# Last attention: head halves instead of key parities in the column tiles of the weighing

## The reference, cut to what matters

```python
q = (x @ Wq).reshape(b, n, 16, 64).transpose(0, 2, 1, 3) * scale
kv = x @ Wkv
k, v = (kv[..., :64], kv[..., 64:])
sim = jnp.einsum('bhid,bjd->bhij', q, k) + bias          # causal mask
attn = jax.nn.softmax(sim, axis=-1)
out = jnp.einsum('bhij,bjd->bhid', attn, v)              # the weighing
out = out.transpose(0, 2, 1, 3).reshape(b, n, 1024)
return out @ Wout + bout                                 # the projection
```

## Time and profile before

| | |
|---|---|
| median of 3 runs | 3847.4 us (3842.58 to 3852.38) |
| the profiled execution | 3845.26 us, span 3843.5 us |
| busy over the span | TensorE 83%, weight loads 45%, VectorE 62%, ScalarE 48%, GpSimd 24% |
| granted TensorE clock, mean | 0.898 |
| weighing, L2367 | 9216 MATMUL records, 324.0 us busy |
| projection of this layer, L2381 | 1024 MATMUL records, 144.0 us busy |
| norm, L2314 | 64 instructions, 151.1 us busy |

### The profile page before, as it was taken

One profiled execution on the slowest core, in us unless ns is written; L12 is line 12 of the kernel. 1 busy time (PEld: TensorE's weight loads), 2 busy tenths in 40 slices (PEclk: granted clock), 3 DMA queues, 4 the chain that ended last, 5 costly groups with the idle time before them and its releaser, 6 DMA issues. The chain is left out here.

```text
span 3843.5 us, 68233 instructions
## 1 busy us (share of the span) xinstructions
PE 3181.4 (83%) x25621; PEld 1748.6 (45%) x25621; DVE 2368.5 (62%) x5084; ACT 1844.5 (48%) x3309; POOL 921.2 (24%) x732
## 2 busy tenths in 40 slices
PE   5748888885759999797699969998888888889899
PEld 2213333331337655573222227763555444555676
DVE  5457777772656455564599942236778777778322
ACT  3214555553226423363289925434555555555444
POOL 1007888894100223000000000001121112212100
PEclk8668999997879899896599969998999988999999
DMA  4112323221033000132422210028444335432100
GB/s 146 41 51 72 106 76 103 79 91 31 12 93 132 2 1 1 45 133 79 144 58 67 68 35 1 1 81 219 122 122 101 108 103 128 122 103 82 31 9 12
DMA packets 229588, 289.46 MB, mean 75 GB/s; under 512 B 44861, under 2 KB 164121, under 8 KB 226950
## 3 DMA queue, kind: packets, MB, share of 16 engines
q1 hardware_dynamic: 229303, 285.61, 25.0%
HBM read 229.49 MB, written 56.55 MB: 74 GB/s over the span
## 5 line engine op out<-in xcount | busy, mean ns | idle before, releaser
L1169 POOL TENSOR_TENSOR l0aa_e<-l0aa_e,l0aa_et 128x512 f32<-128x512 f32 x432 | 538.1, 1274 | 139.1 <-ACT l0aa_e L1311 139.1
L2407 ACT ACTIVATE l1ba_sg<-l1ba_sg,l1ba_mn 128x128 f32<-128x128 f32 (+7 forms) x512 | 394.1, 771 | 303.4 <-DVE l1ba_mn L2451 302.4
L2451 DVE CUSTOM_DVE_ANT_0 l1ba_sg<-l1ba_pS,l1ba_tab 128x128 f32<-128x128 f32 (+7 forms) x512 | 369.0, 745 | 167.4 <-PE l1ba_pS L2347 90.1
L2347 PE MATMUL l1ba_pS<-l1b_k,l1ba_qs 64*128 64x448 f32 (+7 forms) x2048 | 372.2, 470 | 103.5 <-DMA l1ba_qs<-l1b_qd 64.9
L1342 DVE TENSOR_REDUCE l0aa_low<-l0aa_pP 128x8 f32<-128x1024 f32 x288 | 342.2, 1220 | 164.4 <-PE l0aa_pP L1193 163.6
L2460 DVE STREAM_TRANSPOSE l1ba_pT<-l1ba_sg 128x1024 f32<-128x1024 f32 (+3 forms) x344 | 367.1, 1067 | 35.7 <-PE l1ba_pO L2367 32.3
L1311 ACT ACTIVATE l0aa_e<-l0aa_pS 128x512 f32<-128x512 f32 x432 | 257.0, 595 | 259.5 <-PE l0aa_pS L1226 152.7
L2367 PE MATMUL l1ba_pO<-l1ba_pT,l1ba_v 32*64 32x256 f32 x9216 | 324.0, 397 | 5.5 <-ACT l1ba_y L2422 4.6
L319 PEld LDWEIGHTS f_pY<-l_w,f_hT 128*128 128x128 f32 x2048 | 268.1, 192 | 123.8 <-issue 118.8
L2314 POOL TENSOR_TENSOR l1ba_co<-l1ba_co,l1ba_rb 128x1024 f32<-128x1024 f32 x64 | 151.1, 2360 | 709.6 <-ACT l1ba_co L2415 676.7
L2817 ACT ACTIVATE l1aa_e<-l1aa_e 128x1536 f32<-128x1536 f32 x192 | 284.6, 1484 | 43.2 <-DVE l1aa_e L2858 25.9
(11 more groups left out here) (398 smaller groups left out, 5008.1 us busy)
## 6 DMA issues: line engine op xcount, KB each, us to landing
f_wB<-l0f_weights SPq DMA_DIRECT2D x16, 2048.0 KB, 7.2
l1ba_qs<-l1b_qd SPq DMA_DIRECT2D x128, 256.0 KB
l1ba_tab<-l1b_table SPq DMA_DIRECT2D x64, 512.0 KB
l1ba_rb<-l1b_rdd SPq DMA_DIRECT2D x64, 512.0 KB
l0aa_et<-l0a_table SPq DMA_DIRECT2D x16, 1536.0 KB
l1b_qd<-l1bp_part SPq DMA_DIRECT2D x64, 256.0 KB, 2.3
l0aa_et<-l0a_table SPq DMA_DIRECT2D x16, 512.0 KB
l0aa_qs<-l0a_qd SPq DMA_DIRECT2D x64, 96.0 KB
```

The costliest lines, as they stand in the source:

```text
L1169: nc.gpsimd.tensor_tensor(es, es, t, ALU.mult).then_inc(multiplied, 1)
L2347: ins = nc.tensor.matmul(pS[n % 2][:, at:at + half], qs[lo:lo + HALF, r % 2, i + k, :], ks[lo:lo + HALF, key:key + half], start=True, stop ...
L2407: nc.scalar.activation(row, row, ACT.Exp, bias=mn[:, r % 2, i + k:i + k + 1], scale=-1.0, accum_out=den[:, r % 2, i + k:i + k + 1]).then_i ...
L2451: nc.vector.tensor_tensor_reduce(row, scores, bias, 1.0, 3e38, ALU.add, ALU.min, mn[:, r % 2, h:h + 1]).then_inc(m_done, 1)
```

## The change

The column tiles of the weighing now hold two halves of the round's heads (0 to 3 and 4 to 7) and not two halves of the keys. Both column tiles take the same values and stream the 128 columns of their own four heads, so a key block takes 8 matmuls of 128 columns where a pair of key blocks took 8 of 256. `co` then has 4 head pairs of 128 columns instead of 8 heads, with one head of a pair on each half of the partitions. `rb` and `wo` follow: `rb` is loaded by two DMAs, one for each half of the partitions with that half's heads, and `wo` by four. The projection contracts a pair of heads in each of 4 matmuls. The pieces of the weighing are now counted in key blocks and not in pairs of them.

```diff
+    HP = HG // 2
-    def pairs(r):
-        return width(r) // Q // 2
+    def key_blocks(r):
+        return width(r) // Q
...
-        co, rb = sb("co", [P, 2, HG, P]), sb("rb", [P, HG, P])
+        co, rb = sb("co", [P, 2, HP, P]), sb("rb", [P, HP, P])
-        wo, bo = sb("wo", [P, 2 * HG, DIM]), sb("bo", [P, DIM])
+        wo, bo = sb("wo", [P, 2 * HP, DIM]), sb("bo", [P, DIM])
...
-                    sp.wait_ge(r_in, (r - 1) * 16)
+                    sp.wait_ge(r_in, (r - 1) * 32)
...
-                sp.dma_start(rb[:].rearrange("p h q -> p (h q)"), rdd[r % 2:r % 2 + 1].broadcast_to([P, HG * P])
-                             ).then_inc(r_in, 16)
+                for part in (0, 1):
+                    sp.dma_start(rb[part * HALF:(part + 1) * HALF].rearrange("p h q -> p (h q)"),
+                                 rdd[r % 2:r % 2 + 1, part * HP * P:(part + 1) * HP * P].broadcast_to([HALF, HP * P])).then_inc(r_in, 16)
...
-            for lo in (0, HALF):
-                sp.dma_start(wo[lo:lo + HALF], D["L1_attn_b_Wout"].rearrange("(h p) d -> p h d", p=HD)).then_inc(w_in, 16)
+            for hg in (0, 1):
+                for part in (0, 1):
+                    row = (hg * HG + part * HP) * HD
+                    sp.dma_start(wo[part * HALF:(part + 1) * HALF, hg * HP:(hg + 1) * HP],
+                                 D["L1_attn_b_Wout"][row:row + HP * HD, :].rearrange("(h p) d -> p h d", p=HD)).then_inc(w_in, 16)
...
-                for s in range(lo, hi):
+                for j in range(lo, hi):
                     for a in range(STRIPS):
                         for part in (0, 1):
-                            j = 2 * s + part
-                            ins = nc.tensor.matmul(pO[a][part * HALF:(part + 1) * HALF, 0:HG * Q],
+                            ins = nc.tensor.matmul(pO[a][part * HALF:(part + 1) * HALF, 0:HP * Q],
                                                    v4[a * Q:(a + 1) * Q, group_of(r)[0] % 2, (SEQ - width(r)) // Q + j, :],
-                                                   rows[a * Q:(a + 1) * Q, :, j * Q:(j + 1) * Q],
-                                                   start=(s == 0), stop=(s == pairs(r) - 1), skip_group_check=True)
+                                                   rows[a * Q:(a + 1) * Q, part * HP:(part + 1) * HP, j * Q:(j + 1) * Q],
+                                                   start=(j == 0), stop=(j == key_blocks(r) - 1), skip_group_check=True)
...
-                for h in range(HG):
-                    ins = nc.tensor.matmul(pO[BANKS[0]][:, 0:DIM], co[:, r % 2, h, :],
-                                           wo[:, group_of(r)[1] * HG + h, :], start=(h == 0), stop=(h == HG - 1), skip_group_check=True)
+                for k in range(HP):
+                    ins = nc.tensor.matmul(pO[BANKS[0]][:, 0:DIM], co[:, r % 2, k, :],
+                                           wo[:, group_of(r)[1] * HP + k, :], start=(k == 0), stop=(k == HP - 1), skip_group_check=True)
...
-                        weigh(r, (n - first) * pairs(r) // units, (n - first + 1) * pairs(r) // units)
+                        weigh(r, (n - first) * key_blocks(r) // units, (n - first + 1) * key_blocks(r) // units)
...
-                    nc.scalar.activation(co[:, r % 2, :, a * Q:(a + 1) * Q], pO[a][:, 0:HG * Q].rearrange("p (h q) -> p h q", q=Q),
+                    nc.scalar.activation(co[:, r % 2, :, a * Q:(a + 1) * Q], pO[a][:, 0:HP * Q].rearrange("p (h q) -> p h q", q=Q),
```

More of the change, by code:

```diff
@@ L2311, in norm @@
                 pool.wait_ge(o_out, STRIPS * (r + 1))
-                pool.wait_ge(r_in, (r + 1) * 16)
+                pool.wait_ge(r_in, (r + 1) * 32)
                 rows = co[:, r % 2].rearrange("p h q -> p (h q)")
@@ L2322, in add @@
                 nc.gpsimd.tensor_tensor(xs, xs, y[:, r % 2], ALU.add).then_inc(x_done, 1)
-            pool.wait_ge(w_in, 48)
+            pool.wait_ge(w_in, 80)
             rows = x[:, GROUP_BLOCKS:GROUP_BLOCKS + BLOCKS, :]
@@ L2362, in weigh @@
                 rows = pT[r % 2][:, 0:HG * width(r)].rearrange("p (h w) -> p h w", w=width(r))
-                for s in range(lo, hi):
+                for j in range(lo, hi):
                     for a in range(STRIPS):
                         for part in (0, 1):
-                            j = 2 * s + part
-                            ins = nc.tensor.matmul(pO[a][part * HALF:(part + 1) * HALF, 0:HG * Q],
+                            ins = nc.tensor.matmul(pO[a][part * HALF:(part + 1) * HALF, 0:HP * Q],
                                                    v4[a * Q:(a + 1) * Q, group_of(r)[0] % 2, (SEQ - width(r)) // Q + j, :],
-                                                   rows[a * Q:(a + 1) * Q, :, j * Q:(j + 1) * Q],
-                                                   start=(s == 0), stop=(s == pairs(r) - 1), skip_group_check=True)
-                if hi == pairs(r):
+                                                   rows[a * Q:(a + 1) * Q, part * HP:(part + 1) * HP, j * Q:(j + 1) * Q],
+                                                   start=(j == 0), stop=(j == key_blocks(r) - 1), skip_group_check=True)
+                if hi == key_blocks(r):
                     ins.then_inc(pv_done, 1)
```

## The result

The change made the kernel slower: 3877.1 us (median of 5 runs, 3866.1 to 3887.1) against 3845.5 us, a ratio of 1.0083 with a 95% interval of 1.0055 to 1.0112. The forecast was 3775 us, faster. The profiled execution of the changed kernel took 3877.07 us, span 3875.3.

The account below looks back on a forecast made before the run. TensorE was taken to bound the kernel, VectorE close behind; -67 + 6 + 3 - 3 - 12 - 4 + 5 = -72 us from 3845.3 gave 3773, forecast as 3775 us, range 3748 to 3835.

Parts of the forecast that it names:

- What bounds the kernel: TensorE fullest, VectorE next and level in wide units; the projection on the path by nearly its whole length.
- The projection: Projection on TensorE goes from 8 to 4 matmuls a round, 512 of its steps go: -67 us.
- The weighing: Twice the weighing records at half the columns; the wave halves to 0.108 us, sum stays 249 us: +3 us.
- 6.8 ns an instruction: Pace a half wave of the weighing needs, 16 instructions in 0.108 us; a burst's start showed 4.1 ns.
- The instruction rate sets the wave: Rival on the weighing: each of 9216 added records costs 27 ns on TensorE, +249 us, about 3990 us in all; 10%.
- a busy time of 300 us or more for the weighing: Sign on the weighing's line L2367: at this busy time the forecast is wrong by its main step; near 250 expected.
- The two rules of the Trainium skill: Rules against the weighing step: matmul starts at least about 25 ns apart, and an issue floor of some 20 cycles.
- The copies and the norm: Bank copies 0.1 us shorter each, -3 us; norm product 2.36 to 1.27 us; -12 us at groups, -4 at the end.
- -12 us at the group changes: At the start of 7 further head groups, shorter norm and smaller `rb` bring the table sooner: 1.7 us each.
- the 0.4 us that the forecast gave to the shorter copies: At each group change the norm starts 0.4 us sooner behind shorter bank copies.
- the most that the forecast gave to a smaller `rb`: At group changes, with DMA engines full, `rb` brings 0.25 MB less: between 0 and 1.0 us more.
- VectorE's wait for scores: Sign: VectorE's wait for scores from TensorE falls from 90 to about 40 us.

Follow-up runs that it names:

- rest_only: The changed kernel with the weighing of the kernel before (256 columns, half the instructions), all else as changed: 3779.5 us, ratio 0.981.
- split_only: The kernel before with every 256-column weighing matmul made into two of 128 columns, heads 0 to 3 then 4 to 7: 3966.5 us, ratio 1.0293.
- hy_wide: Mixed kernel: new layout in blocks 0, 1, 5, 6 and 7, layout before in 2, 3 and 4; measured level with the kernel before.

## Why the prediction was wrong, step by step

**What bounds the kernel** was right: TensorE's path with VectorE close behind, and rest_only's -66 us fits a projection that stood on it (its copies and norm shrank in the same run).

**The projection** was right in size: 144.0 to 77.2 us in rest_only, -67 as forecast.

**The weighing** is the step that failed: "If the stream sets the wave it halves to 0.108, and the sum stays at 249 us", at +3 us. The wave did halve in the median, to 0.109 us; the mean within bursts is 0.119, where the forecast had 0.109 with its 1 ns. The step failed one level above it: the sum of waves assumes that the instructions for them are there. I asked the right question, whether 6.8 ns an instruction can be held, and answered it with 22 instructions in 0.09 us. That is the rate at which TensorE takes instructions it already has. It says nothing of the rate at which they come from memory, and the half of the trace that does, the instruction queue in the DMA part of the profile, I read and did not use: one page per 7 to 8 us in the wide units before, 4.3 us at the least, twice that need after. That packets come no closer than 3.3 us could not be seen there, since the kernel before never reached it. What could be seen is that the change asks for 256 instructions per 1.74 us inside a burst (16 in 0.109), while the packet alone took about 1.1 us and nothing in the trace showed a shorter turn than 4.3 us. The rival "The instruction rate sets the wave" named the resource and had 10%. Its mechanism was wrong too: it is no slower rate everywhere, +249 us, but holes of 0.5 to 4 us at page ends. The prediction's own sign for this step, a busy time of 300 us or more for the weighing, came with 379.1, but it was set too low to say much: the kernel before has 324.0 for waves that sum to 249.

The two rules of the Trainium skill, by the earlier trace rows and now by the changed kernel: matmul starts at least 25 ns apart ("TensorE: Matmul & The Clock Gate", section "Wait — 56ns, not 53.3ns?") does not hold on 8 tiles, where undisturbed bursts come to 0.22 / 16 = 14 ns. "Runtime: NRT & Kernel Launch", section "Instruction fetch mechanics", says that a sequencer loads 16 KiB blocks of 256 instructions through its own DMA queue, and the 16384-byte packets agree. It also says that fetching stays hidden since dispatch is slower than the fill, and that fails here: TensorE took an instruction in some 4 ns, and 46 times in the changed kernel it stood empty until 2.3 to 3.1 us after the packet of its next page had started.

**What the holes cost.** Over rest_only the stretch of the changed kernel is longer by 949.5 - 841.9 = 107.6 us. The page-end residue holds 81.1 - 3.4 = 77.7 of it. For the other 30 there are two candidates: the longer waves, an estimated 15 us, and the low clock, which lasts 164.5 us against 107.0, 58 more; TensorE's work there takes up to double, so up to 29 us. I did not isolate either. Nor is it shown that the holes bring the low clock: 9 of its 29 stretches begin within 5 us of a hole's start, and such windows cover 24% of the time, 7 of 29 by chance.

**The copies and the norm.** The sizes were right: 275 ns a copy, 1.27 us a norm. So was the -12 us at the group changes. From the norm's start to the table's first use the seven changes take 13.56 us in the mean before (13.04 to 14.15) and 12.10 in rest_only (11.81 to 12.90): -1.46 us each, -10 us in all, before the 0.4 us that the forecast gave to the shorter copies ahead of it. The change shown in the earlier trace rows is one of the quickest of before. A usual one in rest_only, with the wait of VectorE for the table over all seven, which was 65.3 us:

```profile
3183.12 1.27 POOL L2319 TENSOR_TENSOR l1ba_co<-l1ba_co,l1ba_rb 128x512 f32<-128x512 f32 x1 [8.11 <-ACT l1ba_co L2420]
3184.46 1.11 SPq L2279 DMA_DIRECT2D l1ba_rb<-l1b_rdd  x2
...
3185.62 2.64 SPq L2257 DMA_DIRECT2D l1ba_qs<-l1b_qd  x4
...
3188.31 2.16 SPq L2248 DMA_DIRECT2D l1ba_tab<-l1b_table  x4
...
3195.00 1.22 DVE L2456 CUSTOM_DVE_ANT_0 l1ba_sg<-l1ba_pS,l1ba_tab 128x1024 f32<-128x1024 f32 x1 [7.05 <-DMA l1ba_tab<-l1b_table]
```

```profile
DVE l1ba_sg L2456 <- DMA l1ba_tab<-l1b_table: 48.4, 7, 7.9
```

The norm gave 1.1 us. The two `rb` loads took 1.11 us to issue and not 0.70, for a load onto 64 partitions issues in 0.54 us in the median where one onto 128 took 0.34; that took back 0.7 us in the mean, since the norm's end and the table's issue now lie 4.0 us apart and not 3.2. From the table's issue to its use it is 1.1 us less (6.9 and not 8.0), a little more than the most that the forecast gave to a smaller `rb`. The whole forecast without its +3 for the weighing, 3845 - 75 = 3770, is 9 us under rest_only's 3779. VectorE's wait for scores, which fell from 90.1 to 54.8 us there and not to about 40, may be a part of it; the rest stays open, and single executions of rest_only spread from 3767 to 3783.

## What to carry to other kernels

Splitting a matmul keeps its columns and doubles its instructions, and instructions have a supply of their own: divide the count of a dense stretch into the pages of the instruction queue and compare the time of a page of 256 with the nearest distance the queue has shown, for the densest burst and not for the mean. Passing that is not enough: 43 of 46 holes came with packets over 3.7 us apart, because the next page's packet started late and its first instruction followed 2.3 to 3.1 us later. A short run of fast starts shows what the engine can take, never what memory can bring. A change with a gain per round and a price per instruction is best applied where the rounds are short: here in 2 blocks of 8. And read a term from all its occurrences: one of seven group changes, taken by itself, would have given -1 us where the seven give -10.

## What the runs showed of the hardware

In unrolled code TensorE's instructions came in 16384-byte packets, never closer than 3.28 us in any of these kernels (3.34 in the changed one, 3.31 in split_only, 3.28 in hy_wide), about 13 ns an instruction. A packet took 1.0 to 1.2 us in the median of each kernel. In the holes the first of its instructions started 2.2 to 3.3 us after its start and 1.1 to 1.8 us after its end, and in the changed kernel the packet had started 0.3 to 13.6 us after TensorE began the page before. Where it ran dry TensorE stood for up to 4.4 us with the releaser "issue" (split_only). One-column matmuls on the 8 tiles cost 10 to 12 ns each, close to a 128-column one (14 ns). On the SyncE queue a load of `rb` onto 64 partitions issued in 0.54 us (median of 128), one onto 128 partitions in 0.34 us (median of 64).
